# A one-core graph layer: bucket ranks and expert-row mixing as products on TensorE, later starts for the tile steps of the gather stage, and later expert weights

## The reference

```python
edge_index = jnp.stack([src, dst])              # 100000 edges, 6250 rows of 256
xn = _layernorm(x)
x = x + gnn(xn, edge_index, edge_weight) + mix(xn)
x = x + ffn(_layernorm(x))
# gnn: h = x + segment_sum(x[dst] * w, src);  relu(h @ W1 + b1) @ W2 + b2
# mix: per head of 32, k = ln(q), v = ln(q), kv = k^T v / N;  q @ kv + q
# ffn: logits = x @ gate_w + gate_b; two of 16 experts, weights by softmax
h = relu(x @ w1[e] + b1[e]);  out_e = h @ w2[e] + b2[e]
y = x + sum of the two experts' rows, each times its weight
out = layernorm(y) * gamma + beta
```

## Time and profile before

| what | value |
|---|---|
| median of 3 runs | 2381.49 us (2380.33 to 2381.5) |
| the profiled execution's own time | 2381.34 us |
| its span | 2379.1 us |
| mean granted TensorE clock | 0.849 |
| busy: PE, DVE, POOL, ACT | 69%, 61%, 58%, 31% |
| block 1 | 0 to 501 us |
| block 2 | 501 to 1719 us |
| block 3 | 1719 to 1742 us |
| block 4 | 1742 to 2265 us |
| block 5 | 2265 to 2379 us |

### The profile page before, as it was taken

The page is one execution under the profiler, slowest core; times in us unless marked ns, Lnnn a source line. Parts: engine busy times, 40 slices in busy tenths (PEclk is TensorE's granted clock), DMA queues, the critical chain, the costliest instruction groups (busy, mean ns, idle before and its releaser), DMA issues. The chain is left out here.

```text
span 2379.1 us, 40341 instructions
## 1 busy us (share of the span) xinstructions
PE 1638.3 (69%) x9284; PEld 1371.2 (58%) x9285; DVE 1453.1 (61%) x4177; ACT 739.9 (31%) x2173; POOL 1391.3 (58%) x1512
## 2 busy tenths in 40 slices
PE   5602788624556887787878777776569999999900
PEld 2202777613555776676766656654468888888800
DVE  8499988637676666666665665654343443434379
ACT  4803789500000344322222222221213333333200
POOL 8001788748876776677777777776225554555400
PEclk9856899856778999898898889888679999999955
DMA  4000011254333444344444444447581111111184
GB/s 153 0 0 16 20 35 34 20 104 134 115 113 89 133 127 120 108 128 120 127 121 125 124 119 125 124 118 98 77 288 57 62 62 57 60 61 61 52 290 149
DMA packets 133498, 233.44 MB, mean 98 GB/s; under 512 B 28775, under 2 KB 85199, under 8 KB 133374
## 3 DMA queue, kind: packets, MB, share of 16 engines
q0 software_dynamic: 56384, 145.17, 22.8%
q1 hardware_dynamic: 49294, 61.00, 8.4%
q10 hardware_dynamic: 27696, 25.83, 3.4%
HBM read 189.48 MB, written 42.43 MB: 97 GB/s over the span
## 5 line engine op out<-in xcount | busy, mean ns | idle before, releaser
L1278 POOL DMA_INDIRECT lower<-xn_rows,lower x864 | 865.0, 1001 | 310.5 <-issue 239.3
L1303 PE MATMUL bank<-lower 128*128 x960 | 342.9, 443 | 145.4 <-SPq L1154 121.3
L1439 DVE TENSOR_TENSOR xh<-xh,bank 128x256 f32 x480 | 199.7, 416 | 285.9 <-PE bank L1304 285.1
L1422 DVE TENSOR_SCALAR lower<-iota_n,lower 128x128 f32<-128x128 f32 x960 | 294.4, 357 | 69.7 <-issue 56.2
L606 POOL DMA_INDIRECT edge_records_sorted<-lower x112 | 200.8, 1793 | 205.1 <-ACT lower L717 174.9
L1304 PE MATMUL bank<-lower 128*128 x960 | 320.5, 419 | 0.0
L1303 PEld LDWEIGHTS bank<-lower 128*128 128x128 f32 x960 | 177.7, 213 | 212.1 <-issue 200.0
L650 PE MATMUL bank<-lower 128*64 128x128 f32 x1568 | 189.8, 285 | 125.1 <-ACT lower L701 120.8
L650 PEld LDWEIGHTS bank<-lower 128*64 128x64 f32 x1568 | 183.6, 145 | 128.8 <-DVE lower L915 121.4
L1834 POOL DMA_INDIRECT expert_rows<-arena,dest_idx x114 | 114.6, 1005 | 213.7 <-DVE arena L1929 196.5
L1920 DVE TENSOR_SCALAR arena<-bank,b_tile 128x128 f32<-128x128 f32 x456 | 128.4, 344 | 178.4 <-PE bank L1863 178.4
(11 more groups left out here) (316 smaller groups left out, 2530.4 us busy)
## 6 DMA issues: line engine op xcount, KB each, us to landing
lower<-xn_rows,lower POOLq DMA_INDIRECT x864
lower<-in_L_ffn_w SPq DMA_DIRECT2D x16, 512.0 KB, 9.7
upper<-in_L_ffn_w SPq DMA_DIRECT2D x16, 512.0 KB, 10.5
xn_rows<-xh SPq DMA_DIRECT2D x7, 896.0 KB, 4.1
arena<-xn_rows ACTq DMA_DIRECT2D x7, 896.0 KB, 5.5
lower<-xn_rows ACTq DMA_DIRECT2D x49, 128.0 KB
xn_rows<-lower ACTq DMA_DIRECT2D x49, 128.0 KB
x_plus_beta<-lower ACTq DMA_DIRECT2D x49, 128.0 KB
```

Of the source, the lines that this page charges most:

```text
L1278: pool.indirect_dma_start(edge_rows[:, t % ROUND, :], None, xn_dram, bass.IndirectOffsetOnAxis(source.bitcast(U32)[:, t:t + 1], 0)).then_i ...
L1303: pe.matmul(sums_at(u), edge_sel[:, 2 * u % ESEL, :], rows_flat[:, ds(at, D)], start=True, stop=False)
L1422: dve.tensor_scalar(edge_sel[:, (2 * u + h) % ESEL, :], iota_n[:], lane[:, at:at + 1], weight_s[:, at:at + 1], ALU.is_equal, ALU.mult).the ...
L1439: dve.tensor_tensor(xh[:, at], xh[:, at], sums_at(u), ALU.add).then_inc(s_acc, 1)
```

## The change

Everything below is made together.

- **Ranks**: the differences, and the sum of the matches, are now products with the identity and its negative on TensorE in bf16. ACT squares from PSUM. POOL has no part in it. The edges are copied once more with columns outermost (`bkt_c`), so that the count products read runs of 28 neighbouring values. The counts of a round follow every fourth distance in TensorE's order.
- **Prefix and masks**: two fills of `restart` on DVE go to POOL, the start positions are no longer copied, and the loop over buckets is written out. The position sum reads PSUM in two halves.
- **Gathering**: `ET` is 858 instead of 864 (429 pairs). Slots start from `slots_from` at every 7.5 units instead of 4.67, never before `done_by + 2`. The head sums take two buffers in turn, with their products at unit +8 instead of +4 and the additions at +13 instead of +9. `stage_h` is one unit earlier and `mark` two later, behind the other work; the last `mark` moves to block 3.
- **Weights**: block 3 loads gamma and the first expert alone; the next three follow in block 4 when the rows of tile 1 have landed.
- **Final**: the two weighted additions are three fp32 products per tile on TensorE into one of 8 PSUM banks: the identity by `xh`, and two diagonals, made by ACT, by the expert rows. DVE reads PSUM. The first groups have 1, 1, 2 and 3 tiles and the last 3, 2, 1 and 1. Rows are loaded 4 groups ahead instead of 3.

```diff
-    ET = -(-(NGRP * ((GC * P + NT * (QE - 1)) // QE)) // (TQ * ROUND)) * ROUND
-    EROUNDS = ET // ROUND
+    ET = -(-(NGRP * ((GC * P + NT * (QE - 1)) // QE)) // (2 * TQ)) * 2
+    ZT = -(-ET // 8) * 8
...
-                pool.memset(rank, 0.0).then_inc(s_local, 1)
-                pool.wait_ge(s_bkt, 1)
-                for d in range(1, GC + 2):
-                    if d < GC:
-                        if d > 3:
-                            pool.wait_ge(s_same, d - 3)
-                        pool.tensor_tensor(later(apart[d % 3], d), later(bkt_f, d), bg2(bkt_f)[:, :, 0:GC - d],
-                                           ALU.subtract).then_inc(s_gap, 1)
-                    if d >= 3:
-                        pool.wait_ge(s_same, d - 2)
-                        pool.wait_ge(s_local, d - 2)
-                        pool.tensor_tensor(later(rank, d - 2), later(rank, d - 2), later(same[(d - 2) % 3], d - 2),
-                                           ALU.add).then_inc(s_local, 1)
...
+                for a, first in ((restart_g, bg(restart_g)[:, :, 0:1]), (restart_b, gb(restart_b)[:, :, 0:1])):
+                    pool.memset(a, 1.0).then_inc(s_poolc, 1)
+                pool.wait_ge(s_poolc, 6)
+                for a, first in ((restart_g, bg(restart_g)[:, :, 0:1]), (restart_b, gb(restart_b)[:, :, 0:1])):
+                    pool.memset(first, 0.0).then_inc(s_restart, 1)
...
+                def differences(d):
+                    if d > 2:
+                        pe.wait_ge(s_gapsq, d - 2)
...
+                        to = bank[2 + 2 * (d % 2) + h][:, 0:hi - lo]
+                        pe.matmul(to, ident_b, bkt_c[:, lo:hi], start=True, stop=False)
+                        mm = pe.matmul(to, minus_b, bkt_c[:, lo - d * NGRP:hi - d * NGRP], start=False, stop=True)
+                    mm.then_inc(s_gap, 1)
+
+                def add_same(d):
+                    pe.wait_ge(s_same, d)
+                    for h, lo, hi in halves_from(d):
+                        mm = pe.matmul(bank[6 + h][:, lo - h * EH:hi - h * EH], ident_b, same[d % 2][:, lo:hi],
+                                       start=False, stop=hi - lo == NGRP)
+                    mm.then_inc(s_local, 1)
...
-                    matched = match[p].rearrange("p (b g j) -> p b g j", g=NGRP, j=GC)
+                    matched = match[p].rearrange("p (b j g) -> p b j g", g=NGRP, j=GC)
                     for c in range(GC):
-                        mm = pe.matmul(bank[p][:, 0:GT * NGRP], upto_b, matched[:, :, :, c], start=c == 0, stop=c == GC - 1)
+                        mm = pe.matmul(bank[p][:, 0:GT * NGRP], upto_b, matched[:, :, c, :], start=c == 0, stop=c == GC - 1)
                     mm.then_inc(s_counted, 1)
...
+                for h in range(2):
+                    cols = slice(h * EH, (h + 1) * EH)
+                    pe.matmul(bank[6 + h][:, 0:EH], ident_b, bkt_c[:, cols], start=True, stop=False)
+                    pe.matmul(bank[6 + h][:, 0:EH], minus_b, bkt_c[:, cols], start=False, stop=False)
+                differences(1)
+                differences(2)
+                for d in range(1, GC):
+                    add_same(d)
+                    if d + 2 < GC:
+                        differences(d + 2)
+                    if d % 4 == 3:
+                        count(d // 4)
+                assert GC // 4 == NR
...
-                    act.activation(later(apart[d % 3], d), later(apart[d % 3], d), ACT.Square).then_inc(s_gapsq, 1)
+                    if d > 2:
+                        act.wait_ge(s_same, d - 2)
+                    for h in range(2):
+                        lo, hi = max(d * NGRP, h * EH), (h + 1) * EH
+                        if lo < hi:
+                            sq_done = act.activation(apart[d % 2][:, lo:hi], bank[2 + 2 * (d % 2) + h][:, 0:hi - lo], ACT.Square)
+                    sq_done.then_inc(s_gapsq, 1)
...
                         act.wait_ge(s_local, d - 2)
-                    act.activation(later(same[d % 3], d), later(apart[d % 3], d), ACT.Relu, bias=1.0, scale=-1.0).then_inc(s_same, 1)
-
+                    act.activation(same[d % 2][:, d * NGRP:], apart[d % 2][:, d * NGRP:], ACT.Relu, bias=1.0, scale=-1.0).then_inc(s_same, 1)
...
+                dve.tensor_copy(bkt_c.rearrange("p (j g) -> p j g", g=NGRP), by_column(bkt_i)).then_inc(s_bkt, 1)
...
-                dve.tensor_scalar(src_i, src_i, P - 1, None, ALU.bitwise_and).then_inc(s_dve, 1)
-                dve.wait_ge(s_dve, n.add())
-                dve.scalar_tensor_tensor(code, dst_i, float(P), src_i, ALU.mult, ALU.add).then_inc(s_dve, 1)
...
+                dve.tensor_copy(ident_b, ident[:]).then_inc(s_upto, 1)
+                dve.tensor_scalar(minus_b, ident[:], -1.0, None, ALU.mult).then_inc(s_upto, 1)
                 dve.tensor_tensor(upto_b, before[:], ident[:], ALU.add).then_inc(s_upto, 1)
...
-                            dve.tensor_scalar(match[p][:, i * EC:(i + 1) * EC], bkt_f, iota_n[:, ds(r * GT + i, 1)], None,
+                            dve.tensor_scalar(match[r % 2][:, i * EC:(i + 1) * EC], bkt_c, iota_n[:, r * GT + i:r * GT + i + 1], None,
...
-                dve.memset(restart, 1.0).then_inc(s_dve, 1)
-                dve.wait_ge(s_dve, n.add())
-                dve.memset(bg(restart)[:, :, 0:1], 0.0).then_inc(s_dve, 1)
-                dve.wait_ge(s_dve, n.add())
-                dve.tensor_tensor_scan(upto, restart, quads_bg, 0.0, ALU.mult, ALU.add).then_inc(s_dve, 1)
+                dve.wait_ge(s_restart, 2)
+                dve.tensor_tensor_scan(upto, restart_g, quads_bg, 0.0, ALU.mult, ALU.add).then_inc(s_dve, 1)
...
-                            dve.tensor_copy(starts[k % 4], start[:, ds((r * GT + k) * NGRP, NGRP)]).then_inc(s_dve, 1)
...
+                        dve.copy_predicated(bg2(pos), bg2(masks[(b - 1) % 4]), start[:, (b - 1) * NGRP:b * NGRP].unsqueeze(2)
+                                            .to_broadcast([P, NGRP, GC])).then_inc(s_dve, 1)
...
+                for h in range(2):
+                    cols = slice(h * GC // 2, (h + 1) * GC // 2)
+                    dve.tensor_tensor(by_column(pos_i)[:, cols, :], by_column(pos)[:, cols, :],
+                                      bank[6 + h][:, 0:EH].rearrange("p (j g) -> p j g", g=NGRP), ALU.add).then_inc(s_dve, 1)
...
-        turn_unit = [max(slots_from + 1 + -(-14 * s // 3), done_by[s + 1] + 2) for s in range(NT)]
+        turn_unit = [max(slots_from + 1 + -(-15 * s // 2), done_by[s + 1] + 2) for s in range(NT)]
...
                 def load(g):
-                    act.dma_start(xn_rows.rearrange("p (t d) -> p t d", d=D),
-                                  xn_dram[ds(g * (GT * P), GT * P), :].rearrange("(t p) d -> p t d", p=P)).then_inc(s_xt, 16)
+                    if g > 1:
+                        act.wait_ge(s_kvmm, g - 1)
+                    act.dma_start(head_rows(g).rearrange("p (t d) -> p t d", d=D),
+                                  xn_dram[g * GT * P:(g + 1) * GT * P, :].rearrange("(t p) d -> p t d", p=P)).then_inc(s_xt, 16)
...
+                    root()
+                    if g < NG - 1:
                         load(g + 1)
...
-                    for f, later in ((keep, T_TURN2), (root2, T_RESIDUAL), (relu, T_HIDDEN), (copy_turned, 0), (stage_h, -1)):
+                for u in range(LAST + 4):
+                    for f, later in ((keep, T_TURN2), (root2, T_RESIDUAL), (relu, T_HIDDEN), (copy_turned, 0), (stage_h, -2)):
...
-                mark(NT - 1)
-                act.wait_ge(s_x2st, 16 * NT)
-                act.wait_ge(s_xn2st, 16 * NT)
+                    if u - 4 in rank_unit[:-1]:
+                        mark(rank_unit.index(u - 4))
+                last_mark.append(mark)
...
-                            if u == heads_from[g] + 4 + k // 2:
+                            if u == heads_from[g] + 8 + k // 2:
...
-                for e in range(WAHEAD):
-                    sp.dma_start(w1_sb[:, e], w1[e].rearrange("(c p) f -> p c f", p=P)).then_inc(s_we[e], 16)
-                for e in range(WAHEAD):
-                    last = min(NT, -(-(e + 1) * FC * D // D))
-                    sp.wait_ge(s_lists, TOPK * last)
-                    sp.dma_start(w2_sb[:, e], w2[e].rearrange("(m p) d -> p m d", p=P)).then_inc(s_we[e], 16)
+                sp.dma_start(gamma_row, row(gamma)).then_inc(s_gamma, 16)
+                sp.dma_start(w1_sb[:, 0], w1[0].rearrange("(c p) f -> p c f", p=P)).then_inc(s_we[0], 16)
+                sp.wait_ge(s_lists, TOPK * FC)
+                sp.dma_start(w2_sb[:, 0], w2[0].rearrange("(m p) d -> p m d", p=P)).then_inc(s_we[0], 16)
...
+                last_mark[0](NT - 1, act)
+                act.wait_ge(s_x2st, 16 * NT)
+                act.wait_ge(s_xn2st, 16 * NT)
...
+                    if e == 0:
+                        sp.wait_ge(s_tok[1], 16)
+                        for later in range(1, WAHEAD):
+                            load_weights(sp, later)
...
```

(29 more changed lines are left out.)

202 lines of the change are left out of this document (113 added, 89 removed).

## The result

The new kernel takes **2253.74 us** (median of 4 runs, 2252.68 to 2256.53); the kernel before took 2380.91 beside it (2374.72 to 2381.5). The ratio is 0.9473, 95% interval 0.9455 to 0.9491: faster, by 127 us. The profiled execution has a span of 2250.9 us and a mean granted clock of 0.886.

The account below looks back on a forecast made before the run. Limits differ by stage: count products behind counting, DVE to 213 us, POOL's gathers in block 2, TensorE in block 4, DVE in block 5. Seven terms sum to 101.5 us off 2381.3, giving 2280 us; range 2250 to 2322.

Parts of the forecast that it names:

- Counting: Ranks and counts: ACT's chain plus waits for count products at 0.13 us; ends at 68 instead of 92.6, -24.5 us.
- the place of the old 0.341: Rival: the count product stays near 0.341 us, counting ends at 109, 2321 us in all; chance 0.10.
- Prefix, masks, positions: Stretch before the sort loop: fills moved to POOL 3.1 us, start-position copies dropped 8.4, position sum 0.1 more; -11.4 us.
- come after DVE's scaling instead of waiting for it: Block 2: head products at unit +8 no longer wait for DVE's scaling; no gain of their own was priced.
- The slots: Block 2: slots every 7.5 units remove 28 of POOL's 30.7 us of waits for SP's releases; bounds 0 and -40.
- The padding: End of block 2's gathers: six gathers fewer, three pairs at 3.45 us each, -10.4 us.
- The tail: Last gather to block 3: the last mark now lies beside DVE's list work, -2.7 us.
- The last units wait for the last pair, whichever it is: End of block 2: the reason given for counting the three dropped padding pairs in full, -10.4 us.
- Block 4: Expert block: tile 1's rows 4.7 us earlier without weights ahead, but 3 MB more loads inside; -2 us, bounds -5 and +3.
- Final block: Block 5: mixing moves from DVE to TensorE, 79 us at mean clock 0.88; 91.5 instead of 114 us, -22.5 us.
- The rival at 1.2 GHz: TensorE stays near 1.2 GHz in the final block: 149 us there, 2337 us in all; chance 0.12.
- more comes off: Rival: no waits in block 2, counting ends at 61, final block near 84; 2253 us; chance 0.09.

Follow-up runs that it names:

- spread_counts: New kernel with each count's 28 products cut into four sevens, one behind each distance: 2475.94 us, ratio 0.9483 to the kernel before on the second chip.
- strided_match: New kernel with match rows back in the order where a count product reads every 28th value: 2304.65 us, ratio 0.9677 to the kernel before.
- heads_early: New kernel with TensorE's head products back at unit +4, additions and kv step moved back too: 2510.18 us, ratio 0.9642 to the kernel before, second chip.
- combined: New kernel with counts in sevens, early weights in list stage, last three marks moved, seven tiles' own final products early: 2488.76 us, ratio 0.9525, third chip.
- old_weights: New kernel with the first four experts' weights all loaded in the list stage, as before: 2476.26 us, ratio 0.9488 to the kernel before, second chip.
- x_twice: New kernel with one TensorE product of each final-block tile made twice: 2515.79 us, ratio 0.9611 to the kernel before on the third chip.

## Why the prediction was right, and where it was off

**Counting, -38.1 for -24.5.** The mechanism was right to the row: each count stands before what ACT needs. The terms of the sum were too large. The count product took 0.090 us, below the low end of 0.095, and not 0.13; the waits were 9.9 us and not 18. ACT's squares were busy for 13.9 us, not 17.9. Most of that is that one square from PSUM lies under the line of the earlier trace rows, 0.49 us for 392 elements where the line gives 0.55 (40 of them come to 15.2 us); the rest is the overlap of the two halves of one distance. The relus are 14.3 (forecast 14.8). spread_counts shows that the 9.9 us were the counts' doing, and strided_match the price of the order: 0.342. The forecast gave the place of the old 0.341 a chance of 0.10 and said 41 us for it; against the kernel as measured it is 51. The Trainium skill ("SBUF — State Buffer", section "Door 1: The DMA port swizzle") says that reads within one 16-byte line go at full rate and that each step to a new line costs extra. The two runs agree with its direction: 0.090 us with neighbouring values, 0.342 with a step of 56 bytes.

**Prefix, masks, positions, -14.0 for -11.4.** The sum came out near for other reasons than those given. The stretch up to the loop over buckets (137.6, now 94.0) lost 5.5 us for the 3.1 of the fills; 2.0 of them are a shorter wait for TensorE before the first step (7.03, now 5.02). The copies were priced at their 8.4 busy us, but they overlapped the masks: a bucket takes 1.24 us instead of 1.33, which is 4.2 us over 49. The loop gave 4.7 more that the forecast did not have, since the six places where a pass of the old loop ended and the next began held 0.78 us each. The position sums cost 0.7 us more, not 0.1.

**Gathering.** The step that failed is the sentence that the head products "come after DVE's scaling instead of waiting for it" and its price of nothing. I named the wait and did not look for its length: 92.2 us in seven waits of TensorE, 50.5 of them in 640 to 760, which delay the units, SP's releases and POOL. The stretch gained 14.8 us; heads_early shows the mechanism, though at 30 to 38 us and on other chips. The slots were right as a sum, 26.0 for 28, but only 18 of them are the slots': the other 8 appeared neither with ACT's old order (18.5) nor, but for some 3, with all three edits undone (21), both on chips where this block behaves otherwise. Their cause stays open. The padding was right for POOL (11.3 for 10.4) and wrong for the end. That its pairs are slow because all of their rows are one row of memory was not tried.

**The tail, +5.8 for -2.7.** "The last units wait for the last pair, whichever it is" was the clue, and it argued against the sum: fewer pairs of padding leave more units waiting for that one. Before, one unit ran behind the last landing; now four start in 4.6 us. From the last gather to the start of the last sum it is 17.5 us instead of 12.2. The mark that the change put ahead of ACT's copy of h costs 2 us once, at the last turn; combined, which moved it, had the copy 1.8 us sooner and won 0.5. The last mark's own step into block 3 was right in kind: from the last turned copy to block 3's product it is 22.9 us instead of 24.4.

**Block 4, +1.7 for -2.** The first rows came as early as said (tile 1's at 1647.7, 6.6 us after the block's start, for 11.4). But the loads moved into the block cost more: the share of the transfers in its first 59 us is 0.89, and with them in the list stage the block took 1.1 to 3.3 us less in old_weights and 4.7 to 5.6 less in combined. The bounds held for this profile, whose +1.7 is the mildest: the same stretch in the other four traces of the first chip would give +2.2 to +4.2.

**Final block, -28.9 for -22.5.** The limit passed to TensorE as forecast, 69.4 us busy at a mean clock of 0.90; the forecast had 79 at 0.88. A pass took 0.216 us, not 0.236. The 5 us for the cold start were there (the first seven products took 0.84 to 1.02 us each, at a clock of 0.50 until about 2175), the coupling nearly not. The rival at 1.2 GHz, 149 us, did not come: the trace has 1.00 from 2176 to 2240, with one wait of 7.9 us for rows, at the start. The rule that was named for it (the Trainium skill, "TensorE: Matmul & The Clock Gate", section "HAM oscillation") speaks of a wait for transfers behind every short burst. There were no such waits between these products, so this block does not test it.

So the time is that of the rival "more comes off" (2253, chance 0.09), and two of its three parts came as it said: block 2 without POOL's waits, and the final block at 84.6 us from its start where it said 84. Counting ended at 54.5 where it said 61. That the sum agrees within 1 us is luck: counting, the prefix stretch and the gathers gave some 14 us more than the rival had, and the tail, block 4 and the final block took 14 back.

## What to carry to other kernels

When an edit moves a product later "so that it need not wait", look up how long it waited and who is queued behind it: a wait of 13 us on an engine that feeds a ring is not free because it is off the chain shown. Rounding work down at the end of a pipeline is worth only what the last consumer gains; count how many of its steps hang on the last item. Long accumulations in a shared queue should be cut into pieces no longer than the slack of the engine that waits behind them, here 7 products of 0.09 us instead of 28. And an operation that overlaps its neighbours is worth what each turn of the loop gets shorter, not its own busy time: here 0.09 us and not 0.17.

## What the runs showed of the hardware

**The order in which an operand is read.** 28 products of 196 bf16 columns: 2.52 us when each reads neighbouring values, 9.58 when it reads every 28th, and then no more at a granted clock of 0.50 than at 0.80; the kernel before had 1.00 with the same 0.341.

**Three chips, one stage that differs.** The same program took 2381, 2606 and 2615 us on three chips (the kernel before). In the variants of the new kernel the difference is nearly all in block 2: with the new head products and slots the 858 gathers took 1119 to 1120 us on the first chip and 1334 to 1353 on the others, while counting (54.1 and 54.0) and the final block (90.2 and 89.6) agree. A single gather step is 1.25 us on all. Each chip was used at one time only, so whether it is the chip or the moment is not shown. POOL's waits in 1000 to 1500, first of the new kernel on the first chip, then of x_twice on the third:

```profile
POOL lower L1309 <- issue: 106.9, 351, 0.3
POOL lower L1309 <- SPq L1178: 14.0, 46, 0.3
```

```profile
POOL lower L1309 <- SPq L1178: 114.3, 53, 6.3
POOL lower L1309 <- issue: 90.5, 258, 1.8
```

and ACT's, of x_twice:

```profile
ACT lower L1245 <- remote: 57.8, 13, 9.3
ACT std L1250 <- issue: 50.4, 6, 9.2
```

ACT stands for 4 to 9 us with nothing of this core named as what it waits for, which it does not do on the first chip; TensorE waits for ACT, and POOL for TensorE. What holds ACT there stays open.
